# A two-layer attention kernel: when the second copies of the keys are made, and who normalises the last pair of heads

## Chip, cores and metric

The kernel runs on one core of a Trainium2 chip. The metric is the time of one execution in microseconds (us), the median of several executions. The program handles two batches, one after the other, in a loop over `b`; each batch passes through both layers.

## What is computed

Each layer is an attention and a mixture of experts, both behind a layer norm with learned shifts and gates. The change lies in the attention of the second layer, which the reference states as follows (T is 1024 rows, 16 heads of 64 columns):

```
keys, queries, values = residual @ W_key + b, residual @ W_query + b, residual @ W_values + b
scores = einsum('bknh,bqnh->bnqk', keys, queries) / sqrt(H)
scores = where(q_idx < k_idx, EPS, scores)          # masked scores are 1e-10, not minus infinity
probs = softmax(scores, axis=3)
weighted = einsum('bnqk,bknh->bqnh', probs, values)
out = einsum('bqnh,nhe->bqe', weighted, W_output) + Bias_output
x = x + ga * out
```

## The kernel before

The second attention works through 8 pairs of heads, p = 0 to 7, per batch. There is no scheduler: each engine has its own program, written out by hand as a function `pair(p)` (one for TensorE, one for ScalarE, one for VectorE) or a loop (GpSimd), and the engines meet at semaphores that count up. An instruction that waits holds back everything behind it on its engine.

What one pair does, by engine (PE is TensorE, ACT ScalarE, DVE VectorE, POOL GpSimd):

- PE: for 8 tiles of 128 keys, t = 0 to 7, and two heads, `scores(p, t, h)` (L945 and L948). Each head has two PSUM banks for its scores, so `scores(p, t, h)` waits until the exponents of tile t - 1 of that head are done. Between them stand `values(p, t)` (L965), the score maxima of the next pair, `maxima(p + 1, ...)` (L905, L908; 24 units, two banks), its projections (L880, L883, L891), `turn_maxima` (L917), and, after `scores(p, 1, 1)`, `denominators(p - 1)` (L989) for the pair before.
- ACT: `exponents(p, t, h)` (L1541) from PSUM to the tile store (printed as EE or att_in). The ACT program also makes the high parts of the projections (L1502, L1515, L1516), the masked row (L1531), `raw_out(p - 1)` (L1548), `inverse(p - 1)` and `second_k(p + 1)`. `inverse` turns the denominators into their reciprocals by a logarithm (L1556) and an exponential (L1558), 128x1024 each, in the buffer `lnd`, which the profile prints as xn. `second_k` (L1522) copies the high parts of the next pair's keys, 64x1024 for each head (KB from KA, KD from KC); the first reader of these copies is `scores(p + 1, 0, 0)` at the start of the next pair.
- DVE: the reductions of the maxima (L1969), `diagonal(p, t)` (L1994), which replaces the masked half of the diagonal block of each exponent tile, the low parts of the projections (L1944, L1956, L1957), `top(p + 1)` (L1976, L1978), which ends the maxima, and `row_a`. `turn_maxima(p + 1)` on PE waits for L1978.
- POOL: the running sum of the exponents into Esum (L2326, then L2335 for each tile), which starts once PE has read the sum before, and, behind tile 3, `normalise(p - 1)` (L2305): the pair's output in U times the reciprocals, in two halves of 128x512.

After the last pair PE adds up the output projection, `output_of_pair` (L860, 8 tiles of 128 columns), for pairs 0 to 6, then runs `denominators(7)`. ACT runs `inverse(7)`, POOL `normalise(7)`, and PE ends with `output_of_pair(7)`, which releases the residual on DVE (L1728).

## Time and profile before

| | |
|---|---|
| median of 3 runs | 2258.28 us (2254.77 to 2260.71) |
| profiled execution | 2256.03 us, span 2254.2 us |
| PE busy | 1987.2 us (88%) |
| DVE busy | 1439.8 us (64%) |
| ACT busy | 970.6 us (43%) |
| POOL busy | 573.6 us (25%) |

Times in the rows are microseconds from the start of the span. The profiled execution takes 1.8 us more than its span, for what lies around it. The second attention of batch 0 runs from about 690 to 1051 us, that of batch 1 from about 1803 to 2164 us. Busy shares are averages over both layers and say little of one stage.

### The profile page before, as it was taken

Reading aid. Unit: us, or ns where it says so; the run is one execution under the profiler, and the core shown is the slowest. Engines: PE = TensorE matmul, PEld = TensorE weight load, DVE = VectorE, ACT = ScalarE, POOL = GpSimd, SP = SyncE. Lnnn points to the kernel's source line nnn. Section 1 sums busy time; section 2 is a strip of 40 time slices with the busy share of each in tenths; the row PEclk is TensorE's granted clock in tenths of the full one; section 3 lists DMA queues with packets and bytes.
Section 4 is the critical chain, followed back from the end, with each engine's and each line's share of the span. In section 5 each row is a group of like instructions: output and inputs, shape, how many; then the busy total and the mean of one; then the engine's idle time right before and its main releaser. Section 6 shows DMA issues by size and latency. Waiting matters only on the chain.

```text
span 2254.2 us, 31789 instructions
## 1 busy us (share of the span) xinstructions
PE 1987.2 (88%) x10080; PEld 1177.1 (52%) x10080; DVE 1439.8 (64%) x2432; ACT 970.6 (43%) x1358; POOL 573.6 (25%) x543
## 2 busy tenths in 40 slices
PE   6899999996997999997779999999969889999975
PEld 3444444443784555556644444444438755555554
DVE  6677788866317776852377777778662377777432
ACT  2444454441224666561234444544413246656411
POOL 0000000000001787884120000000000037797831
PEclk7999999998886999997969999999979779999977
DMA  3366665678000000000514666666760000000015
GB/s 92 81 152 156 146 147 143 141 162 242 5 1 10 5 6 6 1 1 29 157 37 116 143 148 143 149 151 152 172 201 1 1 10 10 2 6 1 1 61 149
DMA packets 84846, 187.99 MB, mean 83 GB/s; under 512 B 17697, under 2 KB 46754, under 8 KB 83106
## 3 DMA queue, kind: packets, MB, share of 16 engines
q1 hardware_dynamic: 83650, 183.76, 32.5%
q0 software_dynamic: 1024, 2.10, 0.3%
q8 instruction: 88, 1.44, 0.3%
q14 instruction: 84, 0.69, 0.1%
HBM read 178.47 MB, written 8.91 MB: 83 GB/s over the span
## 4 chain that ended last, share of the span: by engine, by line
PE 62%; DVE 15%; issue 11%; ACT 6%; DMA 3%; SPq 1%; POOL 1%; DVEq 0%; ACTq 0%; POOLq 0%
PE PS L794 9%; PE PS L766 5%; PE PS L730 5%; PE PS L905 3%; DVE mx L1836 3%; PE PS L965 3%; PE PS L945 3%; PE PS L751 3%; PE PS L756 3%; PE PS L1136 3%; PE PS L948 2%; PE PS L1191 2%; DMA V<-weight_rows 2%; PE PS L860 2%; DVE mrow L1969 2%
## 5 line engine op out<-in xcount | busy, mean ns | idle before, releaser
L1836 DVE TENSOR_REDUCE mx<-PS 128x8 f32<-128x512 f32 x512 | 329.6, 684 | 178.3 <-PE PS L730 167.3
L2335 POOL TENSOR_TENSOR Esum<-Esum,EE 128x512 f32<-128x512 f32 (+3 forms) x320 | 337.8, 1084 | 14.7 <-POOL Esum L2335 10.1
L1865 DVE TENSOR_TENSOR EE<-EE,V 128x1024 f32<-128x1024 f32 x256 | 302.7, 1217 | 47.2 <-DMA V<-weight_rows 46.4
L1457 ACT ACTIVATE EE<-PS 128x1024 f32<-128x1024 f32 x256 | 260.1, 1024 | 143.6 <-PE PS L756 141.7
L2289 POOL TENSOR_TENSOR U<-xn,norm_aff 128x1024 f32<-128x1024 f32 x2 | 4.7, 2354 | 1073.0 <-DVE QA L2260 1073.0
L794 PE MATMUL PS<-EE,Vlater 128*64 128x512 f32 x1024 | 252.8, 612 | 9.6 <-ACT U L1423 8.3
L1969 DVE TENSOR_REDUCE mrow<-PS 128x1 f32<-128x512 f32 (+3 forms) x384 | 202.6, 550 | 84.6 <-PE PS L908 65.6
L730 PE MATMUL PS<-KA,QA 128*128 128x512 f32 x512 | 203.3, 451 | 28.2 <-DVE mx L1836 21.9
L751 PE MATMUL PS<-QA,KA 128*128 128x512 f32 x512 | 185.3, 443 | 0.0
L1541 ACT ACTIVATE EE<-PS 128x1024 f32<-128x1024 f32 (+2 forms) x192 | 137.8, 738 | 103.8 <-PE PS L948 101.6
L756 PE MATMUL PS<-QB,KB 80*128 80x512 f32 x512 | 163.6, 401 | 0.0
L730 PEld LDWEIGHTS PS<-KA,QA 128*128 128x128 f32 x512 | 97.5, 195 | 126.3 <-DVE mx L1836 84.9
L1994 DVE COPY_PREDICATED EE<-consts,F 128x256 f32<-128x256 int32 x96 | 93.1, 969 | 69.0 <-ACT EE L1541 69.0
L965 PE MATMUL PS<-EE,V 128*64 128x512 f32 (+3 forms) x640 | 131.2, 522 | 0.0
L794 PEld LDWEIGHTS PS<-EE,Vlater 128*64 128x64 f32 x1024 | 61.6, 137 | 117.5 <-issue 91.8
L766 PE MATMUL PS<-EE,consts 128*32 128x512 f32 x1024 | 117.0, 597 | 0.8 <-DVE QA L1813 0.8
L751 PEld LDWEIGHTS PS<-QA,KA 128*128 128x128 f32 x512 | 92.0, 193 | 42.7 <-issue 26.8
L756 PEld LDWEIGHTS PS<-QB,KB 80*128 80x128 f32 x512 | 98.4, 192 | 22.3
L905 PE MATMUL PS<-KA,QA 128*128 128x512 f32 (+1 forms) x192 | 89.0, 463 | 19.4 <-DVE mrow L1969 14.3
L2326 POOL TENSOR_TENSOR Esum<-F,consts 128x1024 f32<-128x1024 f32 x32 | 62.2, 1965 | 107.6 <-PE PS L989 75.3
L905 PE MATMUL PS<-KC,QC 128*128 128x512 f32 (+1 forms) x192 | 84.5, 440 | 0.6 <-DVE mrow L1969 0.2
L945 PE MATMUL PS<-QA,KA 128*128 128x512 f32 (+1 forms) x192 | 67.8, 408 | 12.9 <-ACT EE L1541 11.6
(306 smaller groups left out, 3311.9 us busy)
## 6 DMA issues: line engine op xcount, KB each, us to landing
V<-weight_rows SPq DMA_DIRECT2D x512, 256.0 KB, 5.5
EE<-in_w SPq DMA_DIRECT2D x48, 192.0 KB, 2.8
V<-in_Wg SPq DMA_DIRECT2D x4, 1024.0 KB, 6.3
EE<-in_Wu SPq DMA_DIRECT2D x4, 1024.0 KB, 11.6
EE<-in_Wd SPq DMA_DIRECT2D x4, 1024.0 KB, 13.6
sorted_out<-U SPq DMA_DIRECT2D x12, 256.0 KB, 3.2
wo<-in_wo SPq DMA_DIRECT2D x5, 512.0 KB, 3.7
wq_s<-in_wq SPq DMA_DIRECT2D x17, 128.0 KB, 2.8
```

The lines of the kernel that those rows point to most:

```text
L730: pe.matmul(banks(5 + x % 2, BANK), Q_HIGH[u][:, t * P:(t + 1) * P], KA[g % 2][:, half * BANK:(half + 1) * BANK], start=True, stop=True).t ...
L751: pe.matmul(banks(own, hi - lo, lo), KA[g % 2][:, t * P:(t + 1) * P], Q_HIGH[u][:, lo:hi], start=True, stop=False)
L756: mm = pe.matmul(banks(own, hi - lo, lo), KB[g % 2][0:krows, t * P:(t + 1) * P], Q_LOW[u][0:krows, lo:hi], start=False, stop=True)
L766: mm = pe.matmul(PS[32 * j:32 * j + 32, 4 * BANK:5 * BANK], chunk_sum[:, a, :], EE[i % 2][:, 2 * a + odd, half * BANK:(half + 1) * BANK], ...
L794: mm = pe.matmul(PS[HD * half:HD * half + HD, 7 * BANK:8 * BANK], V0[i // GH % 2][:, t, :], EE[i % 2][:, t, half * BANK:(half + 1) * BANK] ...
L905: mm = pe.matmul(banks(4 + h, hi - lo), M1[h][p % 2][:, t * P:(t + 1) * P], S1[h][p % 2][:, lo:hi], start=True, stop=not own)
L965: mm = pe.matmul(PS[HD * h:HD * h + HD, 6 * BANK + lo:6 * BANK + hi], V1[g % 2][:, t, at:at + HD], e_tile(t)[:, h, lo - t * P:hi - t * P], ...
L1457: act.activation(EE[i % 2][:, t, :], banks(2 * (t % 2)), ACT.Exp, scale=QSCALE).then_inc(s["p2_exp"], 1)
L1836: dve.tensor_reduce(mx[:, t, half * 8:half * 8 + 8], banks(5 + x % 2, BANK).rearrange("p (c k) -> p c k", c=8), AX, ALU.max).then_inc(s["p ...
L1865: dve.tensor_tensor(EE[i % 2][:, t, :], EE[i % 2][:, t, :], weight_ring[a % 2][:, odd, :], ALU.mult).then_inc(p3_mul, 1)
L1969: dve.tensor_reduce(mrow1[:, h, t, half:half + 1], banks(4 + h, width), AX, ALU.max).then_inc(s["mx_red"], 1)
L2335: ins = pool.tensor_tensor(Esum[:, h, lo:hi], Esum[:, h, lo:hi], e_tile(t)[:, h, lo - t * P:hi - t * P], ALU.add)
```

## The change

Two edits. On ACT, `second_k(p + 1)` moves from in front of the exponents of tile 3 to behind those of tile 4, in front of those of tile 5. And the normalisation of the last pair of a batch is done in two halves of 512 columns: ACT takes logarithm and exponential of the first half, then of the second; DVE does the two multiplications in place of POOL; PE runs the last `output_of_pair` as 4 tiles behind each half. Semaphores `u_norm`, `u_inv` and `den_ln` count 9 steps a batch instead of 8 (`NORMS`). POOL still normalises pairs 0 to 6.

```
+NORMS = PAIRS + 1
...
-            def output_of_pair(p, first, last):
+            def output_of_pair(p, first, last, tiles=range(NT)):
...
-                for t in range(NT):
+                for t in tiles:
...
                 output_of_pair(PAIRS - 2, False, False)
                 denominators(last)
-                pe.wait_ge(s["u_norm"], n0 + PAIRS)
-                output_of_pair(PAIRS - 1, False, True).then_inc(s["o_full"], 1)
+                for half in range(2):
+                    pe.wait_ge(s["u_norm"], b * NORMS + PAIRS + half)
+                    mm = output_of_pair(last, False, True, range(4 * half, 4 * half + 4))
+                mm.then_inc(s["o_full"], 1)
...
+                    if p < PAIRS - 1:
+                        act.activation(lnd, banks(6), ACT.Ln).then_inc(s["den_ln"], 1)
+                        act.wait_ge(s["den_ln"], m + 1)
+                        act.activation(lnd, lnd, ACT.Exp, scale=-1.0).then_inc(s["u_inv"], 1)
+                    else:
+                        for half in range(2):
+                            part = lnd[:, half * BANK:(half + 1) * BANK]
+                            act.activation(part, banks(6 + half, BANK), ACT.Ln).then_inc(s["den_ln"], 1)
+                            act.wait_ge(s["den_ln"], m + half + 1)
+                            act.activation(part, part, ACT.Exp, scale=-1.0).then_inc(s["u_inv"], 1)
...
                     if prev:
                         inverse(p - 1)
-                    if follows:
-                        second_k(p + 1)
                     exponents(p, 3, 0)
                     exponents(p, 3, 1)
                     exponents(p, 4, 0)
                     exponents(p, 4, 1)
+                    if follows:
+                        second_k(p + 1)
                     exponents(p, 5, 0)
...
+                dve.wait_ge(s["u_raw"], 1 + n0 + PAIRS)
+                dve.sem_inc(s_held, 1)
+                dve.wait_ge(s["u_norm"], b * NORMS + PAIRS - 1)
+                dve.sem_inc(s_held, 1)
+                for half in range(2):
+                    part = slice(half * BANK, (half + 1) * BANK)
+                    dve.wait_ge(s["u_inv"], b * NORMS + PAIRS + half)
+                    dve.tensor_tensor(U[:, PAIRS - 1, part], U[:, PAIRS - 1, part], lnd[:, part],
+                                      ALU.mult).then_inc(s["u_norm"], 1)
                 dve.wait_ge(S[1]["o_full"], 1 + b + 1)
...
-                normalise(b * PAIRS + PAIRS - 1, PAIRS - 1)
```

ACT in pair 1 before, from the last exponent of tile 2 to those of tile 3; xn is `lnd`, the rows of registers compute what the next instruction waits for:

```order
L1541 ACTIVATE EE<-PS 128x768
L1556 ACTIVATE xn<-PS 128x1024
L1558 ACTIVATE xn<-xn 128x1024
L1520 ISA
L1522 ACTIVATE KB<-KA 64x1024
L1522 ACTIVATE KD<-KC 64x1024
L1537 REGISTER_ALU
L1538 REGISTER_ALU
L1539 REGISTER_ALU
L1541 ACTIVATE EE<-PS 128x640
```

The same place now, to behind the exponents of tile 4:

```order
L1544 ACTIVATE EE<-PS 128x768
L1561 ACTIVATE xn<-PS 128x1024
L1562 ISA
L1563 ACTIVATE xn<-xn 128x1024
...
L1544 ACTIVATE EE<-PS 128x640
...
L1544 ACTIVATE EE<-PS 128x512
L1523 ISA
L1525 ACTIVATE KB<-KA 64x1024
L1525 ACTIVATE KD<-KC 64x1024
```

The two copies now stand behind four more exponents (two of 128x640, two of 128x512), with nothing else moved.

DVE at the end of the second attention before, from the diagonal of tile 7 of the last pair to the residual:

```order
L1994 COPY_PREDICATED att_in<-consts,F 128x256
L1728 ISA
L1728 TENSOR_TENSOR xn<-PS,mod 128x1024
L1729 TENSOR_TENSOR x<-x,xn 128x1024
L1702 BN_STATS stats<-x 128x6 x8
```

And now:

```order
L2005 COPY_PREDICATED att_in<-consts,F 128x256
L2086 REGISTER_ALU
L2088 ISA
L2092 REGISTER_ALU
L2093 TENSOR_TENSOR U<-U,xn 128x512
L2092 REGISTER_ALU
L2093 TENSOR_TENSOR U<-U,xn 128x512
L1739 ISA
L1739 TENSOR_TENSOR xn<-PS,mod 128x1024
```

DVE has gained the two multiplications, between its last diagonal and the residual. PE at the same end, before:

```order
L965 MATMUL PS<-att_in,V 64x128 x2
L860 MATMUL PS<-wo,U 128x128 x8
L986 REGISTER_ALU
L989 MATMUL PS<-Esum,ones_cols 64x512 x4
L860 MATMUL PS<-wo,U 128x128 x8
```

And now:

```order
L861 MATMUL PS<-wo,U 128x128 x8
L987 REGISTER_ALU
L990 MATMUL PS<-Esum,ones_cols 64x512 x4
L1111 REGISTER_ALU
L861 MATMUL PS<-wo,U 128x128 x4
L1111 REGISTER_ALU
L861 MATMUL PS<-wo,U 128x128 x4
```

The last eight tiles are two groups of four, each behind a wait of its own.

## Rows read from the trace of the kernel before

**Rows 1.** Chain that ended last, in pair 4 of batch 0: start us, us, what.

```profile
897.31 1.04 ACT KB L1522
898.35 0.95 ACT KD L1522
```

**Rows 2.** Waits for L1541 by instruction waiting: us, times; both batches.

```profile
PE PS L945: 11.6, 14
```

**Rows 3.** Timeline, PE, pair 0, then pair 4: start, us, operation, idle before.

```profile
741.03 0.33 PE L905 MATMUL PS<-KA,QA 128*128 128x128 f32 x1
...
741.24 0.48 PE L945 MATMUL PS<-QA,KA 128*128 128x512 f32 x1
...
898.61 0.33 PE L905 MATMUL PS<-KA,QA 128*128 128x128 f32 x1
...
899.94 0.50 PE L945 MATMUL PS<-QA,KA 128*128 128x512 f32 x1 [0.93 <-ACT EE L1541]
```

**Rows 4.** Timeline, ACT: pair 4, then tile 5 of pair 6.

```profile
899.21 1.27 ACT L1541 ACTIVATE EE<-PS 128x640 f32<-128x640 f32 x2
...
906.26 1.09 ACT L1541 ACTIVATE att_in<-PS 128x384 f32<-128x384 f32 x2 [4.30 <-PE PS L948]
...
985.63 1.09 ACT L1541 ACTIVATE att_in<-PS 128x384 f32<-128x384 f32 x2 [3.41 <-PE PS L948]
```

**Rows 5.** Timeline, DVE and POOL, end of the maxima in pair 4; then pair 0.

```profile
914.69 0.98 DVE L1994 COPY_PREDICATED EE<-consts,F 128x256 f32<-128x256 int32 x1
...
915.32 1.47 POOL L2305 TENSOR_TENSOR U<-U,xn 128x512 f32<-128x512 f32 x1
916.74 1.26 POOL L2335 TENSOR_TENSOR Esum<-Esum,EE 128x512 f32<-128x512 f32 x1
...
917.10 0.94 DVE L1978 TENSOR_TENSOR mx<-mtop,consts 128x16 f32<-128x16 f32 x1
...
757.97 0.19 DVE L1978 TENSOR_TENSOR mx<-mtop,consts 128x16 f32<-128x16 f32 x1
```

**Rows 6.** Timeline, pair 6 and the denominators behind it: PE, POOL, PE.

```profile
982.42 0.50 PE L905 MATMUL PS<-KA,QA 128*128 128x512 f32 x1 [0.83 <-DVE mrow L1969]
...
1003.35 0.87 POOL L2335 TENSOR_TENSOR Esum<-Esum,att_in 128x128 f32<-128x128 f32 x2 [0.16 <-POOL Esum L2335]
...
1005.65 1.94 PE L989 MATMUL PS<-Esum,ones_cols 128*64 128x512 f32 x8
```

**Rows 7.** Timeline, all engines, the end of batch 0's second attention.

```profile
1040.08 1.94 PE L989 MATMUL PS<-Esum,ones_cols 128*64 128x512 f32 x8
...
1042.06 1.02 ACT L1556 ACTIVATE xn<-PS 128x1024 f32<-128x1024 f32 x1 [2.83 <-PE PS L989]
1043.12 1.06 ACT L1558 ACTIVATE xn<-xn 128x1024 f32<-128x1024 f32 x1
1044.35 2.48 POOL L2305 TENSOR_TENSOR U<-U,xn 128x512 f32<-128x512 f32 x2 [5.15 <-ACT xn L1558]
...
1046.89 3.78 PE L860 MATMUL PS<-wo,U 128*128 128x128 f32 x16 [4.87 <-POOL U L2305]
```

**Rows 8.** Groups by shape: count, busy us, mean ns, idle before.

```profile
L1541 ACT ACTIVATE EE<-PS 128x512 f32<-128x512 f32 x16 | 9.4, 597 | 3.3 <-PE PS L948 2.9
...
L2005 DVE TENSOR_TENSOR V<-PS,bv_s 128x512 f32<-128x512 f32 x32 | 20.4, 677 | 0.0
```

**Rows 9.** Timeline, PE, two waits in other stages.

```profile
1076.55 0.70 PE L1242 MATMUL PS<-hT,EE 128*128 128x512 f32 x1 [2.25 <-DVE EE L2173]
...
1209.83 0.38 PE L737 MATMUL PS<-consts,mx 128*16 128x128 f32 x1 [2.74 <-DVE mx L1836]
```

**Rows 10.** Stretches: length, busy by engine, PEclk (1.00 full), DMA share, GB/s.

```profile
1046.89:1050.67 3.78, 3.78 (x16) 3.49 (x16) 0.00 (x0) 0.00 (x0) 0.00 (x0) 0.50 0.00 0
1076.55:1079.55 3.00, 3.00 (x15) 2.04 (x16) 0.98 (x1) 0.00 (x0) 2.39 (x3) 1.00 0.66 192
1209.83:1212.83 3.00, 3.00 (x12) 1.43 (x14) 2.67 (x3) 1.01 (x1) 0.00 (x0) 0.50 1.04 236
```

More of the change, by code:

```diff
@@ L958, in values @@
                         if p >= 1:
-                            pe.wait_ge(s["den_ln"], n)
+                            pe.wait_ge(s["den_ln"], b * NORMS + p)
                         pe.wait_ge(s["v_out"], 1 + (g0 + g + 1) * 2)
@@ L1105, in attention1 @@
                     values(last, t)
-                pe.wait_ge(s["u_norm"], n0 + PAIRS - 1)
+                pe.wait_ge(s["u_norm"], b * NORMS + PAIRS - 1)
                 output_of_pair(PAIRS - 2, False, False)
                 denominators(last)
-                pe.wait_ge(s["u_norm"], n0 + PAIRS)
-                output_of_pair(PAIRS - 1, False, True).then_inc(s["o_full"], 1)
+                for half in range(2):
+                    pe.wait_ge(s["u_norm"], b * NORMS + PAIRS + half)
+                    mm = output_of_pair(last, False, True, range(4 * half, 4 * half + 4))
+                mm.then_inc(s["o_full"], 1)
             def mixture(b):
@@ L1553, in inverse @@
                     act.wait_ge(s["den_ps"], 1 + n + 1)
+                    m = b * NORMS + p
                     if p >= 1:
-                        act.wait_ge(s["u_norm"], n)
-                    act.activation(lnd, banks(6), ACT.Ln).then_inc(s["den_ln"], 1)
-                    act.wait_ge(s["den_ln"], n + 1)
-                    act.activation(lnd, lnd, ACT.Exp, scale=-1.0).then_inc(s["u_inv"], 1)
+                        act.wait_ge(s["u_norm"], m)
+                    if p < PAIRS - 1:
[8 more added lines that the diff above has]
+                            act.activation(part, part, ACT.Exp, scale=-1.0).then_inc(s["u_inv"], 1)
                 def row_b(p):
@@ L2300, in normalise @@
                     pool.sem_inc(s_held, 1)
-                    pool.wait_ge(s["u_inv"], n + 1)
+                    pool.wait_ge(s["u_inv"], b * NORMS + p + 1)
                     pool.sem_inc(s_held, 1)
```

## The prediction, made before the changed kernel ran

> **What bounds the kernel now.** The page's busy shares (PE 88%) say only that PE leads on average, so I read the stage that is changed, in five views.
>
> First the chain of waits inside one pair of the second attention. `inverse` on ACT is followed on that chain by both second copies, at 897.31 and 898.35 [rows 1], about 2.0 us of work that nobody reads before the next pair. Then the waits by line: PE stood idle 11.6 us in 14 waits on L1541 before L945 [rows 2]. The timeline shows twelve of these to be one wait of 0.93 us, the one before `scores(p, 4, 0)` in pairs 1 to 6 of both batches; pair 4 stands for them [rows 3]. The other two are 0.19 us each, in pair 7. In pair 0, which has no `inverse`, the same score starts 0.21 us behind the start of the maximum in front of it (741.03 to 741.24); in pair 4 it takes 1.33 us (898.61 to 899.94) [rows 3]. So the delay of PE is 1.12 us, of which the idle figure shows 0.93, since matmuls overlap.
>
> Third, ACT around it. The exponents of tile 3 run 899.21 to 900.48, and ACT then idles 4.30 us before those of tile 5 in pair 4 and 3.41 us in pair 6 [rows 4]. That is room for the copies.
>
> Fourth, what follows until the pair ends: DVE's maxima, then L1978, for which the transposes on PE wait. L1978 takes 0.19 us in pair 0, where POOL is idle, and 0.94 us in pair 4 [rows 5]. There it starts at 917.10, inside a POOL operation that began at 916.74 and takes 1.26, and ends at 918.04, 0.04 behind that operation. The diagonal of tile 6 shows the same: begun 914.69, ended 915.67, behind the POOL boundary at 915.32 [rows 5]. So these DVE operations end behind the end of whichever POOL operation they meet. POOL's own sequence starts with the denominators, before the part that moves. An earlier DVE therefore gains in steps of one POOL operation. Here the boundary before 918.00 (916.74 + 1.26) is 916.79 (915.32 + 1.47), 1.21 us earlier.
>
> The Trainium skill states this as a rule: in "SBUF — State Buffer", section "SBUF: two separate sides", the port pair that VectorE and GpSimd share is an exclusive lock, held for the whole instruction, and the later one blocks. The trace agrees (0.94 against 0.19 us). By the bare idle figure the twelve pairs would give 11.2 us, by this rule 14.5, at one step of 1.21 in each.
>
> Fifth, the end of the stage [rows 7]. Denominators end at 1042.02; logarithm, exponential, two POOL halves (2.48 us) and then 3.78 us of output projection follow in strict sequence, to 1050.67. PE idles 4.87 us in it and comes back at half clock [rows 10].
>
> **The change, part by part.**
>
> Second copies in pairs 1 to 6. The exponents of tile 3 start 1.90 us earlier (899.21 to 897.31, where the first copy stood). Their first result is then there at 898.0, before PE asks, so `scores(p, 4, 0)` starts at 898.82. PE gains 1.12 us. The copies now follow the exponents of tile 4, which end about 900.85, and last until 902.8; tile 5 wants ACT at about 904.9. If that cover were gone they would cost their 2.0 us per pair; it holds with 2 us to spare, in pair 6 with about 0.5. From there PE and DVE run 1.1 to 1.4 us ahead. L1978 would start near 915.85, meets the POOL operation that ends at 916.79, and ends near 916.83 instead of 918.04: 1.21 us. It would still meet that same boundary with as little as 0.31 us of lead (917.10 less 916.79), so the size is robust. Behind it everything up to the next pair follows. Five pairs (1 to 5) in two batches: 10 x 1.21 = 12.1 us.
>
> Pair 6 has no projections to fill PE, and its next wait is on DVE, 0.83 us at 982.42 [rows 6], which goes as well because DVE's diagonal of tile 3 is early too. PE would be 2 us or more ahead; but `denominators(6)` needs POOL's sum, which ends at 1004.22, and now starts at 1005.65 [rows 6]. POOL does not move, so the gain is at most 1.43 less a handoff of 0.05: 1.38 us, twice 2.8. POOL is what is late next.
>
> Pair 0 had no wait on PE (741.24): nothing. Pair 7 has no copies: nothing. Sum of this part 14.9 us.
>
> The last pair. Logarithm of half 0: 0.60 us, by the 128x512 form of L1541 [rows 8], since the 1024 form of L1556 (1.02) costs what L1541's does; the exponential 0.63, with the 0.04 more that L1558 has over L1556 [rows 7]. With a handoff of 0.05 they end at 1043.34. The handoff from ACT takes 0.17 us (1044.18 to 1044.35 [rows 7]), DVE's multiplication 0.68 by L2005 [rows 8], which has the same width with one input in PSUM. Its bounds are 0.19 (L1978, the same kind at 16 columns [rows 5]) and 1.24 (half of POOL's 2.48 [rows 7]). I take 0.68, the row of the same engine and width. Half 0 is ready at 1044.19 and PE, 0.06 later, starts at 1044.25. ACT's second half ends at 1044.53, DVE's at 1045.38, PE's second group starts at 1045.44. At full clock four tiles take half of 3.78/2, 0.95 us plus 0.1 to drain, so PE ends at 1046.5: 4.2 us earlier, 8.4 in both batches. At half clock the eight tiles take 3.78 from 1044.25, to 1048.0: 2.7 us, 5.3 in both.
>
> Which clock? PE's wait would be 2.2 us instead of 4.87. After 2.25 us the clock was full for the next 3 us, after 2.74 us it was half [rows 9, 10]. I take full, by the nearer row.
>
> The page "VectorE: DVE Perf Modes", section "The TRN2 errata", of the Trainium skill gives (N+151)/0.96 for such an fp32 multiplication, an estimate of 0.69 us for 512 columns. By it the sum would change by 0.02 us.
>
> The new waits on DVE queue nothing behind them that is due: DVE has nothing until the residual. POOL loses one pair of instructions that nothing followed.
>
> Sum: 12.1 + 2.8 + 8.4 = 23.3 us. The profiled execution took 2256.03 us, so 2232.7; the median of the runs shown is 2.25 us above it, so I state 2235 against 2258.28.
>
> **The rivals.**
>
> The clock stays at half at the end: 14.9 + 5.3 = 20.2 us, 2238. For it: a wait of 2.2 us lies close to the 2.74 us that was followed by half clock [rows 9], and a second small gap follows between the groups. Chance 0.24.
>
> Two POOL boundaries. If DVE is far enough ahead, L1978 ends one step earlier still. It would have to start before 915.5, where I have 915.85. Ten more steps give 12.1 us more, 35.4 in all, 2223. For it: the diagonals of tiles 4 and 5 also end at POOL boundaries, and each may save a step. Against it: in pair 0, which has the least to wait for, L1978 ends 16.92 us behind the start of that score (758.16 and 741.24), in pair 4 18.10 [rows 3, 5]; so at most 1.12 + 1.18 = 2.3 us can be won, and two steps are 2.42. The lock rule above is what would do this. Chance 0.10.
>
> The copies do nothing: the wait for ACT only turns into one for DVE or for POOL in each pair, as it may where PE waits for the maxima. Only the end remains, 8.4 us (5.3 at half clock): 2250, at worst 2253. For it: the timeline shows DVE without idle time between its diagonal of tile 5 and L1978. Against it: that run starts behind an exponent that PE releases, and it moves with PE. Chance 0.13.
>
> Slower. One mechanism: DVE's shared-port operations after the moved part (the diagonals of tiles 4 to 7, L1978, the casts L1956) meet later boundaries than now. Each lost step costs 1.21 us in ten pairs, 12.1 us. Two lost steps a pair (24.2) cancel the sum of 23.3, three give +13.0 us, 2271. Against it: an operation that comes earlier to a POOL sequence that stands still cannot end later. Only those that now happen to meet a gap can lose. Chance 0.05.
>
> **How the numbers follow.** My forecast has 0.48. About 0.3% (6.8 us) is what a measurement of this kernel can tell from no change, since its three runs span 5.9 us. Forecast, half clock and two boundaries are all faster, 0.82. Of "the copies do nothing" most lies beyond 6.8 us at full clock, 0.09, the rest is no change, with a little for mixtures: 0.05. Slower 0.04, the part of that rival beyond the bound. Faster 0.91. The range takes in the first three cases, 0.82: from 2222 (two boundaries, less 1 for the measurement) to 2243. The upper end is the idle figure alone with the half clock, 11.2 + 5.3 = 16.5 us, 2241.8, plus 1.
>
> **What the profile after would show.** The twelve waits of L945 on L1541 gone, two of 0.19 left. ACT's idle time before tile 5 about 2.3 us instead of 4.30, the copies directly in front of it. L905 in front of `scores(4, 4, 0)` about 154.0 us behind the same place of pair 0, instead of 157.6 (three whole pairs lie between that gain). L1978 still 0.9 us long. In pair 7 PE waiting for POOL, or nearly, before the denominators at about 1.4 us less than now. At the end PE idle 2.2 us, two groups of 0.95 us at a PEclk of 1.00, and DVE's residual 4.2 us sooner after the denominators. The prediction falls if PE is found waiting longer for DVE's maxima than now, if L1978 ends no earlier after the denominators, or if L860 runs at 0.50.

## Result and the profile after

The changed kernel takes 2235.79 us (median of 4 runs, 2234.03 to 2239.64) against 2259.49 (4 runs, 2254.77 to 2261.34): ratio 0.9897, 95% interval 0.9878 to 0.9917, faster. The profiled execution took 2235.18 us, with a span of 2233.3 us against 2254.2.

The page after, the busy line and the TensorE clock in 40 slices:

```profile
PE 1979.2 (89%) x10080; PEld 1176.0 (53%) x10080; DVE 1434.9 (64%) x2436; ACT 971.0 (43%) x1362; POOL 571.0 (26%) x539
...
PEclk7999999998886999998969999999979869999987
```

Nothing in it says where 21 us went: the largest fall of a busy time, PE's, is 8 us. The stage has to be read. Lines have moved: L905 is now L906, L945 L946, L989 L990, L860 L861, L1541 L1544, L1522 L1525, L1978 L1989, L1994 L2005; POOL's L2305 is L2325 and L2335 is L2355. In the kernels of the experiments the same lines stand a few numbers higher or lower again.

Who waited for the exponents L1544, in both batches (us, times):

```profile
  PEld PS L946: 4.7, 8
...
  PE PS L946: 0.4, 2
```

The twelve waits of 0.93 us [rows 2] are gone, two of 0.19 us are left. The timeline shows why. PE in pair 0, then pair 4:

```profile
740.40 0.33 PE L906 MATMUL PS<-KA,QA 128*128 128x128 f32 x1
740.61 0.48 PE L946 MATMUL PS<-QA,KA 128*128 128x512 f32 x1
...
895.11 0.33 PE L906 MATMUL PS<-KA,QA 128*128 128x128 f32 x1
895.32 0.48 PE L946 MATMUL PS<-QA,KA 128*128 128x512 f32 x1
```

Pair 4 now has the same 0.21 us as pair 0, where it had 1.33 [rows 3]. ACT in the same place:

```profile
893.81 1.28 ACT L1544 ACTIVATE EE<-PS 128x640 f32<-128x640 f32 x2
896.07 1.25 ACT L1544 ACTIVATE EE<-PS 128x512 f32<-128x512 f32 x2 [0.98 <-PE PS L949]
897.21 1.04 ACT L1525 ACTIVATE KB<-KA 64x1024 fp32r<-64x1024 f32 x1
898.16 1.05 ACT L1525 ACTIVATE KD<-KC 64x1024 fp32r<-64x1024 f32 x1
901.38 1.10 ACT L1544 ACTIVATE att_in<-PS 128x384 f32<-128x384 f32 x2 [2.17 <-PE PS L949]
```

Exponents of tiles 3 and 4, the two copies, and then 2.17 us of idle time where there were 4.30 [rows 4]: the copies lie in idle time. The end of the maxima, DVE and POOL, and the transposes on PE that wait for them:

```profile
909.38 1.28 POOL L2355 TENSOR_TENSOR Esum<-Esum,EE 128x512 f32<-128x512 f32 x1
909.80 1.17 DVE L2005 COPY_PREDICATED EE<-consts,F 128x256 f32<-128x256 int32 x1
910.61 2.68 POOL L2325 TENSOR_TENSOR U<-U,xn 128x512 f32<-128x512 f32 x2
912.39 0.94 DVE L1989 TENSOR_TENSOR mx<-mtop,consts 128x16 f32<-128x16 f32 x1
913.44 1.03 PE L918 MATMUL PS<-consts,mx 128*33 128x128 f32 x8 [1.11 <-issue]
```

L1989 still takes 0.94 us, but it ends at 913.33, just behind the end of the second L2325 (913.29), where it ended behind the L2335 that follows [rows 5]: one POOL operation earlier. Below, such an end of a POOL operation is called a boundary. Pairs are 38.97 us apart (from the denominators of one to those of the next) instead of 40.2. In pair 7 POOL is what is late, as in rows 6 it was not:

```profile
997.75 0.86 POOL L2355 TENSOR_TENSOR Esum<-Esum,att_in 128x128 f32<-128x128 f32 x2 [0.16 <-POOL Esum L2355]
...
998.67 1.94 PE L990 MATMUL PS<-Esum,ones_cols 128*64 128x512 f32 x8 [1.58 <-POOL Esum L2355]
...
2099.50 3.36 PE L990 MATMUL PS<-Esum,ones_cols 128*64 128x512 f32 x8 [1.58 <-POOL Esum L2355]
```

The same wait of 1.58 us stands in both batches, but in batch 1 the eight products behind it took 3.36 us. The end of batch 0, to compare with rows 7:

```profile
1033.09 1.94 PE L990 MATMUL PS<-Esum,ones_cols 128*64 128x512 f32 x8
...
1035.07 0.60 ACT L1567 ACTIVATE xn<-PS 128x512 f32<-128x512 f32 x1 [2.83 <-PE PS L990]
1035.70 0.63 ACT L1569 ACTIVATE xn<-xn 128x512 f32<-128x512 f32 x1
...
1036.36 0.69 DVE L2093 TENSOR_TENSOR U<-U,xn 128x512 f32<-128x512 f32 x1 [20.26 <-ACT xn L1569]
...
1037.11 3.51 PE L861 MATMUL PS<-wo,U 128*128 128x128 f32 x16 [2.08 <-DVE U L2093]
1037.51 0.69 DVE L2093 TENSOR_TENSOR U<-U,xn 128x512 f32<-128x512 f32 x1 [0.46 <-ACT xn L1569]
```

And the clock in stretches (length, busy time by engine, PEclk):

```profile
1037.11:1040.62 3.51, 3.51 (x16) 3.21 (x16) 0.69 (x1) 0.37 (x1) 0.00 (x0) 0.55 0.00 0
...
2099.50:2102.86 3.36, 3.36 (x9) 0.84 (x9) 0.41 (x1) 0.00 (x0) 0.00 (x0) 0.57 0.00 0
998.67:1000.61 1.94, 1.94 (x9) 0.56 (x9) 0.41 (x1) 0.00 (x0) 0.00 (x0) 1.00 0.00 0
```

The granted clock was 0.55 in the last products, and 0.57 against 1.00 behind the two equal waits for POOL. 1.00 is 2.4 GHz, and 0.50 is 1.2 GHz.

**Where the time came from**, by the starts of the denominators and the last output products, in us for batch 0 and batch 1:

```
                         before           after            gained
pairs 1 to 5             200.08  200.10   194.87  194.86   5.21   5.24
pair 6                    35.05   35.06    33.89   33.88   1.16   1.18
pair 7                    34.43   34.43    34.42   35.81   0.01  -1.38
last denominators to end  10.59   10.59     7.53    7.28   3.06   3.31
stage, sum               280.15  280.18   270.71  271.83   9.44   8.35
```

That is 17.8 us. The spans differ by 20.9 and the medians by 23.7. The rest lies outside these two stretches. In the 14 profiled executions of this study the time outside them varied from 1678.6 to 1697.2 us, and how much of a single difference there belongs to an edit isn't shown. So below, each kernel has its median and ratio, and the length of the two stretches ("stage") from its trace. The stage begins at `denominators(0)`, behind pair 0; and since one trace has its clock drops where they happen to fall, a difference of 1 to 3 us in it can be a drop and not the edit.

### The profile page after: what moved, and what is told of

Read it like the earlier page. It is cut to its first block, busy times and chain, and to the rows that moved or that the text cites. A ratio compares the mean times of both kernels' runs of the same rounds, so it can differ in the third digit from the quotient of the medians.

```text
span 2233.3 us, 31843 instructions
## 1 busy us (share of the span) xinstructions
PE 1979.2 (89%) x10080; PEld 1176.0 (53%) x10080; DVE 1434.9 (64%) x2436; ACT 971.0 (43%) x1362; POOL 571.0 (26%) x539
## 4 chain that ended last, share of the span: by engine, by line
PE 65%; DVE 14%; issue 10%; DMA 3%; POOL 3%; ACT 3%; SPq 1%; DVEq 0%; POOLq 0%; ACTq 0%
PE PS L795 9%; PE PS L767 5%; PE PS L731 5%; PE PS L966 4%; PE PS L906 4%; PE PS L946 3%; DVE mx L1847 3%; PE PS L752 3%; PE PS L949 3%; PE PS L757 3%; PE PS L1139 3%; PE PS L861 2%; PE PS L1194 2%; DMA V<-weight_rows 2%; POOL Esum L2355 2%
## 5 line engine op out<-in xcount | busy, mean ns | idle before, releaser
L2355 POOL TENSOR_TENSOR Esum<-Esum,EE 128x512 f32<-128x512 f32 (+3 forms) x320 | 339.9, 1090 | 15.3 <-POOL Esum L2355 10.1
L1544 ACT ACTIVATE EE<-PS 128x1024 f32<-128x1024 f32 (+2 forms) x192 | 138.1, 739 | 122.3 <-PE PS L949 120.2
L2005 DVE COPY_PREDICATED EE<-consts,F 128x256 f32<-128x256 int32 x96 | 85.8, 894 | 49.8 <-ACT EE L1544 49.7
L906 PE MATMUL PS<-KA,QA 128*128 128x512 f32 (+1 forms) x192 | 89.7, 467 | 18.2 <-DVE mrow L1980 12.6
L906 PE MATMUL PS<-KC,QC 128*128 128x512 f32 (+1 forms) x192 | 84.8, 442 | 0.6
L2337 POOL TENSOR_TENSOR Vlater<-V 128x256 f32<-128x256 f32 x8 | 5.8, 723 | 283.3 <-DVE V L2016 283.3
```

The source lines that it names most:

```text
L906: mm = pe.matmul(banks(4 + h, hi - lo), M1[h][p % 2][:, t * P:(t + 1) * P], S1[h][p % 2][:, lo:hi], start=True, stop=not own)
L2355: ins = pool.tensor_tensor(Esum[:, h, lo:hi], Esum[:, h, lo:hi], e_tile(t)[:, h, lo - t * P:hi - t * P], ALU.add)
```

## Experiments

Measured, all against the kernel before in the same series of runs (its median there 2256 to 2259 us); "stage less" is how much shorter both stretches were together than before, in one trace.

```
                                median (runs)   ratio to before [95%]     stage b0/b1      stage less
changed kernel                  2235.8  (4)     0.9897 [0.9878, 0.9917]   270.71/271.83     17.8
e1 copies only                  2242.8  (6)     0.9922 [0.9901, 0.9944]   273.92/273.89     12.5
e2 end only                     2254.4 (12)     0.9978 [0.9960, 0.9995]   281.91/280.53     -2.1
e3 maximum with one input       2263.0 (12)     1.0008 [0.9988, 1.0028]   281.65/282.77     -4.1
e4 filler at the end            2230.4  (6)     0.9878 [0.9855, 0.9900]   269.45/270.88     20.0
e5 one copy on each side        2237.6  (1)     -                         271.74/271.75     16.8
e6 no small maximum             2264.0 (12)     1.0043 [1.0021, 1.0065]   288.57/286.85    -15.1
e7 POOL relieved                2232.3  (6)     0.9904 [0.9888, 0.9921]   269.17/269.19     22.0
e8 e6 + e7 + filler at the end  2255.1 (12)     0.9997 [0.9973, 1.0020]   281.19/278.21      0.9
e9 whole on DVE                 2235.6  (1)     -                         273.84/273.84     12.7
e10 e6 + filler at the head     2230.9  (6)     0.9892 [0.9859, 0.9926]   271.60/271.34     17.4
e11 e8 + filler at the head     2219.7  (6)     0.9839 [0.9808, 0.9871]   267.39/267.45     25.5
e12 e7 + filler at the end      2226.1  (6)     0.9855 [0.9818, 0.9892]   269.58/269.56     21.2
```

**e1, the copies alone.** The kernel before, with `second_k(p + 1)` behind the exponents of tile 4 and nothing else.

```
-                    if follows:
-                        second_k(p + 1)
                     exponents(p, 3, 0)
...
                     exponents(p, 4, 1)
+                    if follows:
+                        second_k(p + 1)
```

> The kernel before, with only the second copies moved behind the exponents of tile 4; the end of the stage is as before. My theory (the copies are worth one POOL operation in each of pairs 1 to 5, and in pair 6 what POOL leaves): 12 to 15 us faster than before, L1978 one POOL boundary earlier, PE waiting about 1.6 us for POOL before the denominators of pair 6. Rival (the change pays only at the end, and the rest of the difference is other stages): under 5 us faster. The two single edits together should give what the whole change gave, 23.7 us by the medians; if they give about 18, some of it was not theirs.

Measured 2242.8 us. Pairs 1 to 5 are 38.97 us apart (pair 3 39.08), pair 6 takes 33.9, the ends 10.59 as before. The stage gains 6.2 us a batch: the whole effect of the copies, and with it the rival that they do nothing is out.

**e2, the end alone.** The changed kernel with the copies where they were.

```
+                    if follows:
+                        second_k(p + 1)
...
-                    if follows:
-                        second_k(p + 1)
```

> The changed kernel with the second copies back in front of the exponents of tile 3; only the last pair's normalisation by halves stays. My theory: 6 to 7 us faster than before (3.1 to 3.3 in each batch, as the profile after shows, since the clock falls during the last eight output tiles). If the clock stays full it is 8.4, if it is half throughout 5.3. Rival (the end is hidden by something later, such as the loads of the expert weights): 0 to 2 us.

Measured 2254.4 us. The ends took 7.68 and 6.33 us, 2.9 and 4.3 less than before, so e1 and e2 add up to about what the change brings (16.4 and 4.7 us by the medians, 21 of 23.7). But pair 6 took 37.5 us instead of 35.05 and pair 7 36.0 instead of 34.43, which no edit here touches. PE in pair 6, and the clock around it:

```profile
980.83 0.51 PE L906 MATMUL PS<-KA,QA 128*128 128x512 f32 x1 [0.84 <-DVE mrow L1980]
```

```profile
978.00:981.00 3.00, 1.56 (x7) 0.97 (x7) 1.70 (x3) 2.33 (x4) 2.84 (x3) 1.00 0.00 0
981.00:986.00 5.00, 5.00 (x18) 2.12 (x19) 2.72 (x5) 0.31 (x1) 4.84 (x6) 0.66 0.00 0
```

It is the wait of rows 6 (0.83 us there), behind the one of 0.93, and here the clock fell behind it (0.66 over 5 us). The same two waits were in the kernel before, at full clock. In pair 7 the clock fell too, here with no idle time of PE in front of it. So the two traces don't add up as the medians do (12.5 and -2.1 against 17.8 us); the lengthening of pairs 6 and 7, 8 us in both batches, is as large as what is missing.

Pair 3 took 40.19 us here, against 39.52 in the kernel before, whose pairs are written out in the same order. The reason is in the trace before, DVE and POOL at the end of the maxima of pair 3:

```profile
876.90 0.95 DVE L1978 TENSOR_TENSOR mx<-mtop,consts 128x16 f32<-128x16 f32 x1
```

```profile
876.54 1.27 POOL L2305 TENSOR_TENSOR U<-U,xn 128x512 f32<-128x512 f32 x1
```

There the small maximum ended (877.85) behind the second L2305 (877.81), one boundary earlier than in pair 4 [rows 5]. In pair 3 of e2 it ended (876.23) behind the L2355 that follows L2325 (876.19), one boundary later. So a small margin decides which boundary is met, and pair 3 of the kernel before already had most of the step.

**e3, the small maximum with one input.** The two-input maximum with the epsilon row became two `tensor_scalar`, one with a constant for seven tiles, one for the eighth.

```
-                    dve.tensor_tensor(mx1[:, :, 0:33:32].rearrange("p t h -> p h t"), mtop1[:, :, :], const("eps_row").unsqueeze(1).to_broadcast([P, 2, NT]),
+                    wide = mx1[:, :, 0:33:32].rearrange("p t h -> p h t")
+                    dve.tensor_scalar(wide[:, :, 0:NT - 1], mtop1[:, :, 0:NT - 1], EPS_MASK / QSCALE, None, ALU.max)
+                    dve.tensor_scalar(wide[:, :, NT - 1:NT], mtop1[:, :, NT - 1:NT], const("eps_row", NT - 1, NT), None,
```

> The changed kernel, with the last step of the maxima (a 128x16 tensor_tensor with a constant from SBUF) written as two tensor_scalar with one SBUF input each, same values. Theory of the shared port: its 0.94 us is a wait for POOL's operation, so the two take about 0.2 us each, the transposes come 0.5 to 0.7 us sooner in pairs 1 to 6, and the kernel is 4 to 9 us faster than the changed one. Rival (the instruction is slow by itself or by its strided output when the engines are loaded): it still takes 0.9 us or more, no change in time.

Measured 2263.0 us: not the gain that I expected of it. DVE and POOL at the end of the maxima of one pair:

```profile
920.12 0.93 DVE L1990 TENSOR_SCALAR mx<-mtop 128x14 f32<-128x14 f32 x1
920.96 1.30 DVE L1991 TENSOR_SCALAR mx<-mtop,consts 128x2 f32<-128x2 f32 x1
```

```profile
918.34 2.67 POOL L2327 TENSOR_TENSOR U<-U,xn 128x512 f32<-128x512 f32 x2
920.97 1.26 POOL L2357 TENSOR_TENSOR Esum<-Esum,EE 128x512 f32<-128x512 f32 x1
```

Each of the two ends 0.04 us behind the end of a POOL operation (921.05 and 921.01, 922.26 and 922.23), 14 and 2 columns wide, where in pair 0, with POOL's operation ending (759.90) as they begin (759.84 and 759.92), they take 0.18 and 0.22 us. (L1978 in pair 0 before had the same: it began at 757.97, and POOL, which the prediction calls idle there, ended at 758.03.) So the one-input form meets POOL too, and two such instructions end at two boundaries, where one ended at the first of them. My edit was wrong, and the boundary theory came out stronger. The Trainium skill has it in "SBUF — State Buffer", section "Who interferes with whom": copy, cast and `tensor_scalar` can take the shared pair, reductions never do. The trace agrees, and with e6 below on the reduction too.

Not every lost microsecond is a boundary, though. PE now waits 2.3 us for the maxima of the next pair, where it waited 1.11. Two such waits, 40 us apart, had different clocks behind them. The wait in pair 4 of batch 0, and the clock behind it and behind its like in pair 3 (882.16):

```profile
922.36 1.04 PE L918 MATMUL PS<-consts,mx 128*33 128x128 f32 x4 [2.30 <-issue]
```

```profile
922.50:925.50 3.00, 3.00 (x10) 1.99 (x10) 1.22 (x2) 1.06 (x2) 2.84 (x3) 0.50 0.00 0
881.80:885.00 3.20, 2.84 (x14) 1.63 (x16) 1.54 (x3) 1.74 (x3) 3.04 (x4) 1.00 0.00 0
```

The pairs without a drop took 40.1 to 40.2 us, one boundary (1.2 us) more than 38.97. The five with one took 41.5 to 43.1.

**e4, TensorE kept busy at the end.** Eight products of 512 columns into a bank that nobody reads any more, while PE waits for the last normalisation.

```
                 denominators(last)
+                for k in range(8):
+                    pe.matmul(banks(4, BANK), S1[0][last % 2][:, 0:P], M1[0][last % 2][:, 0:BANK], start=True, stop=True)
```

> The changed kernel, with eight matmuls of 512 columns into a bank that nobody reads between the last denominators and the last output tiles, about 1.75 us of PE work in a wait of 2.08 us. Theory of the clock: PE is then idle only 0.3 us, the clock stays full, the last sixteen matmul records take 2.0 to 2.3 us instead of 3.5 and 3.3, and each batch gains about 1.2 us over the changed kernel, 2.4 in all. Rival (the last tiles are slow because they wait for the second half): the clock is full and the end comes no earlier, under 0.5 us.

Measured 2230.4 us. PE at the end, and the stretch of the output products:

```profile
1031.17 2.11 PE L1111 MATMUL PS<-QA,KA 128*128 128x512 f32 x8
...
1033.33 2.31 PE L861 MATMUL PS<-wo,U 128*128 128x128 f32 x16
```

```profile
1033.14:1035.64 2.50, 2.44 (x17) 1.94 (x16) 0.82 (x2) 0.56 (x1) 0.00 (x0) 1.00 0.00 0
```

With work in place of the wait the clock is 1.00 and the end takes 6.34 us in both batches, against 7.53 and 7.28. 10.59 less 6.34 is 4.25, the 4.2 of the prediction. That it is the clock and not something else about the extra products is shown by e5 below, which has none: its PE waited the same 2.08 us at the end, its clock stayed full, and both ends took 6.33 us.

```profile
1039.98:1042.30 2.32, 2.31 (x16) 1.94 (x16) 0.69 (x1) 0.38 (x1) 0.00 (x0) 1.00 0.00 0
```

The seven kernels that have the two halves and no extra products there have 14 batch ends: 4 took 6.33 us and 10 took 7.22 to 7.68. The four with the products (e4, e8, e11, e12) have 8 ends, all of 6.33 to 6.34. So with the products the clock was kept at every end, and without them at some, with nothing in the code to tell which. In the traces they bring 2.2 us (1.20 and 0.94 at the ends). The medians differ by 5.4, and the difference isn't explained.

**e9, whole on VectorE.** The changed kernel with one logarithm, one exponential, one multiplication on DVE and one group of products.

```
-                for half in range(2):
...
-                    dve.tensor_tensor(U[:, PAIRS - 1, part], U[:, PAIRS - 1, part], lnd[:, part],
+                dve.tensor_tensor(U[:, PAIRS - 1, :], U[:, PAIRS - 1, :], lnd, ALU.mult).then_inc(s["u_norm"], 1)
```

> The changed kernel with the last pair's normalisation on VectorE, but whole: one logarithm, one exponential and one multiplication of 128 by 1024, and one group of eight products pairs behind it, instead of halves. It splits the gain at the end of a batch in its two parts. From the start of the last denominators to the end of the last output products the kernel before took 10.59 us and the changed one 7.53 and 7.28. If the engine alone made it (POOL's two-input multiplication of 2.48 us against VectorE's, about 1.35 us for the same columns), the stretch is about 9.4 us, and the halves bring the remaining 2 us. If the halves alone made it, it stays near 10.6 us.

```profile
1037.64 1.23 DVE L2091 TENSOR_TENSOR U<-U,xn 128x1024 f32<-128x1024 f32 x1 [21.16 <-ACT xn L1563]
...
1038.92 3.78 PE L861 MATMUL PS<-wo,U 128*128 128x128 f32 x16 [3.47 <-DVE U L2091]
```

The end took 9.19 us. The engine brought 1.40 (1.23 us for DVE against 2.48 [rows 7], and 0.15 of handoff), the halves 1.66 to 1.91 more, with the clock as it was: here 3.78 us for the output products, 3.51 in batch 0 of the changed kernel.

**e5, one copy on each side.** Head 0's copy ahead of the exponents of tile 3, head 1's behind tile 4.

```
+                    if follows:
+                        second_k(p + 1, (0,))
...
-                        second_k(p + 1)
+                        second_k(p + 1, (1,))
```

> The changed kernel with only one of the two second copies of the next keys behind the fifth exponents; the other stands ahead of the fourth's. So the scores of tile 4, and all ScalarE work behind them, come later by one copy's time less the wait that the bank allows, 0.14 us or more in each pair. The boundary theory (the small maximum ends where a POOL operation ends, and these sit on POOL's own grid) says that the maximum still meets the same boundary: from the start of POOL's second minimum to the end of the maximum 22.38 us as in the changed kernel, and the pairs stay at 38.97. A linear theory (what ScalarE loses, the pair loses) says 39.1 us or more for each of pairs 1 to 5. If the maximum slips to the next boundary, 23.6 us and pairs of 40.2.

In pair 4, the diagonal of tile 6 and the small maximum:

```profile
910.98 1.00 DVE L2007 COPY_PREDICATED EE<-consts,F 128x256 f32<-128x256 int32 x1
...
913.41 0.94 DVE L1991 TENSOR_TENSOR mx<-mtop,consts 128x16 f32<-128x16 f32 x1
```

Pairs are 39.07 us apart, 0.10 more. Counted from the start of POOL's first product into Esum (889.06 after, 889.98 here; the expectation calls these products minima), DVE came to this diagonal 0.26 us later (21.00 against 20.74), the diagonal was 0.17 shorter (1.00 against 1.17), and the maximum ended 0.10 later (24.37 against 24.27). The boundary took up 0.17 of the 0.26. The rest is in POOL's own sequence: its four sums of tile 2 took 4.00 us together where they took 3.87. So the steps are real, but POOL's sequence isn't fixed. That DVE delays POOL as well would explain it, and fits the changed kernel, where of the two equal halves of L2325 the one that began while DVE's diagonal was running took 1.46 us and the other 1.25; it isn't isolated by a run. Of what I had written, neither the unchanged 38.97 nor the reason of the linear theory holds in full. Pair 7 took 36.0 us in both batches, with a clock drop behind no listed wait.

**e6, no small maximum.** The epsilon row is stored once as a third column next to the two column maxima; the reduction writes the result.

```
-        mrow1 = sb("mrow1", [P, 2, NT, 2])
+        mrow1 = sb("mrow1", [P, 2, NT, 3])
...
-                    dve.tensor_reduce(mtop1[:, :, :], mrow1[:, :, :, :], AX, ALU.max).then_inc(s["m_both"], 1)
-                    dve.tensor_tensor(mx1[:, :, 0:33:32].rearrange("p t h -> p h t"), mtop1[:, :, :], const("eps_row").unsqueeze(1).to_broadcast([P, 2, NT]),
+                    dve.tensor_reduce(mx1[:, :, 0:33:32].rearrange("p t h -> p h t"), mrow1[:, :, :, :], AX,
                                       ALU.max).then_inc(s["m_top"], 1)
```

> The changed kernel with the small maximum of the top masks taken out as an instruction of its own: the epsilon row is stored once as a third column beside the two column maxima, and the reduction that stood ahead writes the same result. Everything else is as in the changed kernel. The lock theory says: VectorE's small two-input instruction ends where an operation of POOL ends, 0.91 to 0.94 us instead of its own 0.19, and the diagonal and ScalarE's wait stand behind it. Without it each of pairs 1 to 5 is shorter by the 0.7 to 1.2 us between one POOL boundary and VectorE's own pace, so a pair takes 37.8 to 38.3 us instead of 38.97; pair 6 stays at 33.9, since POOL's own work sets the start of its successor's denominators. Sum: 10 pairs by 0.95 is 9.5 us, 2226 us. Rival A (another wait takes its place, such as the diagonal, which then meets the port one operation earlier): the pairs keep 38.97 and the time stays at 2236 us. Rival B (the copies' order was the whole cause, not the lock): the pairs are shorter by no more than the instruction's free length of 0.19 us, 2234 us.

Measured 2264.0 us: 28 us slower than the changed kernel, which none of the three had. Two things are in the trace. First, the diagonal of tile 7 at the head of the next pair, with POOL:

```profile
801.92 1.28 DVE L2003 COPY_PREDICATED att_in<-consts,F 128x256 f32<-128x256 int32 x1
...
803.04 0.74 POOL L2355 TENSOR_TENSOR Esum<-Esum,EE 128x256 f32<-128x256 f32 x1 [0.16 <-POOL Esum L2355]
```

It takes 1.28 us and ends behind a POOL operation; in the changed kernel it takes 0.45. That is Rival A of the expectation: the reduction now takes 0.20 us beside a busy POOL, the maxima are ready earlier, and the next instruction that needs the port waits for the boundary instead. Second, PE comes early to the next maxima and waits there for DVE (idle 1.07 us at 845.23, 1.08 at 806.37). The clock behind these two waits:

```profile
845.23 0.33 PE L906 MATMUL PS<-KA,QA 128*128 128x128 f32 x1 [1.07 <-DVE QD L1968]
```

```profile
806.50:812.50 6.00, 5.81 (x30) 3.44 (x30) 2.23 (x6) 3.56 (x4) 3.92 (x6) 1.00 0.01 3
845.50:854.50 9.00, 8.80 (x30) 5.00 (x28) 2.35 (x6) 3.77 (x4) 0.00 (x0) 0.62 0.01 2
```

Equal waits, 39 us apart, once 1.00 behind them and once 0.62. From there on each pair of batch 0 up to pair 6 had a drop; three of them took 42.0 to 43.5 us between the transposes. Pair 2, where the wait was met at full clock, took 38.87, and pair 1 took 37.93, which the expectation of e10 below puts down to pair 2. Over both batches of e6 and e8 the heads of pairs 2 to 6 have 20 such waits of 1.06 to 1.10 us: behind 16 the clock fell, behind 4 it did not.

**e10, e6 with TensorE kept busy in that wait.**

```
                     if follows:
+                        pe.wait_ge(s["lo_out"], 8 * (n + 1) + 6)
+                        for k in range(4):
+                            pe.matmul(banks(4, BANK), S1[0][p % 2][:, 0:P], M1[0][p % 2][:, 0:BANK], start=True, stop=True)
                         pe.wait_ge(s["lo_out"], 8 * (n + 1) + 8)
```

> The kernel without the small maximum of the top masks (2264.0 us, slower by 28 us than the changed kernel although its first full pairs took 37.93 us instead of 38.97), with four extra products of 512 columns on TensorE, into a bank that is free then, ahead of the wait for VectorE's low part of QD that begins each pair's next maxima. In the run without them TensorE waits 1.07 to 1.10 us there, and from pair 3 on the granted clock is 0.50 for 3.4 to 5.1 us of lost clock behind it, in pairs that take 42.0 to 43.5 us; in pair 2 the same wait was met at full clock and the pair took 37.93. Theory of the clock: TensorE has work through that wait, its clock stays at 1.00, and pairs 1 to 5 take 37.9 to 38.6 us: 2224 to 2230 us. Rival (the loss is VectorE's late low part of QD, which now meets POOL, and not the clock): the pairs stay at 42 us and more, 2260 us.

```profile
918.98 1.09 PE L1017 MATMUL PS<-QA,KA 128*128 128x512 f32 x4
920.22 0.33 PE L906 MATMUL PS<-KA,QA 128*128 128x128 f32 x1
```

Measured 2230.9 us, 33 us less than e6, by 56 products more that nobody reads. No drop is left in pairs 1 to 6. Pairs are 38.86 us apart: 0.1 below the changed kernel, not the 0.95 that the instruction seemed to cost. So the clock was e6's loss, and with it away Rival A is what remains of e6. Against the changed kernel the stage gains nothing (17.4 us against 17.8): the 5 us between the medians lie elsewhere, 4.4 of them in pair 0, ahead of the stage. From the transposes for pair 0 to `denominators(0)` it took 50.65 and 50.28 us here (50.43 and 50.44 in e11), 52.23 and 53.11 in the changed kernel and 52.28 and 52.19 before: a clock drop at the head of pair 0, which both of these had, is gone.

**e7, POOL relieved.** DVE normalises pairs 5 and 6 during pair 7, with the two multiplications that POOL made (`normalise` on DVE, called a second time for pair 6).

```
-                        if t == 3 and p >= 1:
+                        if t == 3 and 1 <= p < PAIRS - 2:
...
+                    if p == PAIRS - 1:
+                        normalise(PAIRS - 3)
```

> The changed kernel with the normalisations of pairs 5 and 6 of each batch moved from POOL to VectorE, which has idle time in the last pair; POOL keeps pairs 0 to 4. If POOL's own work sets the start of the denominators of pair 6 in the changed kernel, the wait of 1.58 us of TensorE before them goes, the stretch from the denominators of pair 5 to those of pair 6 falls from 33.89 to about 32.5 us, and so do both batches: 2 by 1.4 us, 2233 us, and another 1.7 us where TensorE's clock fell behind that wait. Rival (VectorE's own two operations of 1.3 us are on the path of the last pair's maxima): the stretch from the denominators of pair 6 to those of pair 7 grows by up to 2.6 us from 34.42 and the time is 2236 to 2240 us.

Measured 2232.3 us. From the denominators of pair 5 to those of pair 6 it takes 32.31 us instead of 33.88: the 1.58 us of PE's wait for POOL. Pair 7 stays at 34.41 in both batches. The rival's cost did not come, though two of DVE's multiplications took 3.2 to 3.4 us together beside POOL.

**e8, the edits of e6, e7 and e4 together.**

> The changed kernel with three edits together: the small maximum of the top masks folded into the reduction ahead of it, pairs 5 and 6 normalised on VectorE, and eight extra products of 512 columns on TensorE into a finished bank while it waits for the last normalisation. Extra work only, the output is the same. If the three gains are independent the sum is 9.5 us of the first, 2.8 to 5 of the second and 5 of the third (2235.8 less 2230.4, as measured with the filler alone): 2217 to 2219 us. If the first finds another wait in its place, 2227 us.

Measured 2255.1 us, beyond both. The ends take 6.33 us and pair 6 32.34 (33.29 in batch 1), as the parts promised, but the heads of the pairs lose the clock as in e6.

**e11, e8 with the four products of e10 at the head of each pair; e12, e7 with the eight products of e4 at the end.** Both are made of edits shown above.

> All edits together: no small maximum of the top masks, pairs 5 and 6 normalised on VectorE, eight extra products at the end of a batch, and the four extra products at the head of each pair. Without the last it took 2255.1 us, with the granted clock at 0.50 behind the head of five pairs of batch 0 and four of batch 1. If the clock is the loss, 2214 to 2220 us; if not, 2250 us.

> The changed kernel with pairs 5 and 6 of a batch normalised on VectorE (2232.3 us alone) and eight extra products at the end of a batch (2230.4 us alone). The first took about 1.55 us from the stretch between the denominators of pair 5 and pair 6, the second 1.2 and 0.95 us from the end of the batches. If they add up: 2235.8 less 3.5 less 5.4 is 2226.9 us. Rival: both gains were the same clock drop kept away, and the time is 2230 us.

e11 takes 2219.7 us, ratio 0.9839, the shortest of all. Its pairs are 38.87, 32.35 and 34.41 us apart, its ends take 6.34, and no clock drop is left between pair 1 and the end of the stage. e12 takes 2226.1 us by the median, as the sum said (2226.9). But its trace doesn't show that sum: the stage is no shorter than in e7 (21.2 against 22.0). The ends gained 2.6 us, and pair 7, with 36.0 us in both batches, lost 3.2 to a drop at 1013 us in batch 0 and its like in batch 1, behind no wait that the timeline lists. So the rival of that expectation isn't out, and what makes a drop is not settled.

## Why the prediction was right

It said 2235 us, and 2235.79 was measured. The mechanism of the copies and that of the halves were right. The full clock at the end was not: the prediction named L860 at 0.50 as a sign against it, and in batch 0 it ran at 0.55. All three sizes were too large, and the total hides that.

- **PE's wait before `scores(p, 4, 0)`.** Right. All twelve are gone, and the copies lie in ACT's idle time (2.17 us left, 2.3 predicted). e1 alone shows the gain.
- **One POOL boundary a pair, 10 x 1.21 = 12.1 us.** Right in kind: in pair 4 the maximum ends one operation earlier. Mis-sized: 10.45 us. Pairs 1, 2, 4 and 5 gained 1.24, 1.13, 1.09 and 1.24, but pair 3 only 0.51, since its maximum had met the earlier boundary before (under e2). I had multiplied by five what I had read in pair 4. The offset that I gave to check it, 154.0 us from pair 0 to pair 4, came out at 154.7.
- **Pair 6, bounded by POOL, 2.8 us.** Right. PE waits 1.58 us for POOL before `denominators(6)`, and e7 shows that POOL is the bound there. The size is 2.34, because POOL's sum ended 33.83 us behind the denominators of pair 5 and not 33.62: POOL did move, by 0.2 us. Not foreseen was that in batch 1 the clock would fall behind this wait, 1.4 us.
- **The end, 8.4 us at full clock.** This was the largest miss of a term: 6.4 us. PE's wait was 2.08 us (2.2 predicted) and DVE's half 0.69 (0.68 predicted). An estimate of 0.69 also comes from the Trainium skill's page "VectorE: DVE Perf Modes", section "The TRN2 errata", whose formula is stated there for an fp32 addition; the trace agrees for the multiplication. But the clock was 0.55 in batch 0, and L861 took 3.51 us where I had two groups of 0.95. "I take full, by the nearer row" is the step that failed; the rival at half clock (5.3) was nearer. e4 gives the full term. One row of 2.25 us and one of 2.74 could not decide it: behind the same wait of 2.08 us the clock stayed full at 4 ends and fell at 10 (under e4).
- **Two boundaries.** Did not come. L1989 started at 912.39, and the boundary before, the end of the first L2325, was at 912.07 (910.61 and 1.46): 0.32 us too late for a second step. I had 0.35, from a boundary at 915.5 that no row gives; by rows 5 it stood at 915.32, which makes 0.53. e10 shows more: even a maximum that needs no port wins only 0.1 us a pair, because the next instruction with a port then waits.
- **Slower.** Did not come by the change. e3 shows that a lost boundary does cost what was said, 1.24 us in each pair. The clock drops cost more, as e6 shows, and the prediction had no such rival within the pairs.

The terms as measured make 10.45 + 2.34 + 6.37 - 1.37 = 17.8 us, against 23.3 predicted. The medians differ by 23.7. About 6 us of that lie outside the stretches that the change touches, or in drops that a single trace of each kernel doesn't show; an excess of the same sign, 2.7 to 11.3 us, stands between the medians and the stretches of the six other kernels of the table that were timed and faster than 0.995. In e10 and e11 about 3.5 us of it are in pair 0; what the rest is stays open. So the total came within 1 us by luck: with the stretches alone it would have been 2258.3 less 17.8, 2240.5 us, inside the range of 2222 to 2243 but not at 2235.

## What to carry to other kernels

Where two engines share a port, count in whole operations of the one that keeps its own pace: a start earlier by any amount gives a step or nothing, and when one such wait is taken away, look for the next instruction that will meet the same boundary before promising its gain. Before multiplying a step by the number of loop turns, read it in every turn. When a change leaves TensorE a wait of 1 to 2 us, price it twice, with and without a clock drop behind it, and try a few products that nobody reads in that place: here this was worth 2.2 us at the ends (in the traces) and 33 us at the heads of the pairs, where removing the small maximum had opened the waits. Where one trace has a drop and another has none, compare the pieces without drops before crediting an edit.

## What was not expected of the hardware

- The granted clock fell behind 16 of 20 waits of 1.06 to 1.10 us (e6 and e8), behind one of two of 1.58 us (after) and behind one of 2.30 us in e3 (0.50 in the 3 us that follow), and stayed at 1.00 behind equal waits elsewhere in the same executions. Behind the 1.58 us a drop lengthened eight products from 1.94 to 3.36 us. In e12 and e5 it also fell in pair 7 behind no listed wait. What else decides it, the runs don't show.
- `tensor_scalar` in fp32 from SBUF to SBUF meets POOL's operations like a two-input instruction (0.93 and 1.30 us against 0.18 and 0.22), a reduction of 48 columns does not (0.20).
- POOL's operations are not of fixed length beside DVE: the four sums of tile 2 took 3.87 us after and 4.00 in e5, and two halves of L2325 with the same shape 1.46 and 1.25. That DVE's use of the port is the reason is likely but not isolated.
